# A vision tower with a product-key attention: four dense and four gathered heads in 64 slots, for three and a half and 56

## The reference, cut to what matters

```python
def _pk(x, Wq_pk, pk_keys):                    # 8 heads, 64 keys on each of two sides
    sim = einsum('pbnhd,pkhd->pbnhk', q, pk_keys)
    scores, idx = top_k(sim, 16)               # per side
    index = idx0[:, None] + 64 * idx1[None, :] # 256 pairs
    score = scores0[:, None] + scores1[None, :]
    final_scores, pk_idx = top_k(score, 16)    # 16 rows of 4096 per token and head
    return softmax(final_scores), index[pk_idx]
k = einsum('bnhk,bnhkd->bnhd', kv_scores, keys_table[ind])
v = einsum('bnhk,bnhkd->bnhd', kv_scores, values_table[ind])
sim = einsum('bihd,bjhd->bhij', q, k)          # causal, softmax over 256 tokens
out = softmax(sim) @ v                         # then @ Wo
```

## Time and profile before

| | |
|---|---|
| time, median of 3 runs | 17584.85 us (17558.91 to 17630.44) |
| the profiled execution's own time | 17614.6 us |
| its span, first to last instruction | 17612.8 us |
| granted TensorE clock, mean | 0.823 |
| PE matmuls busy | 13397.9 us (76%) |
| DVE busy | 10470.6 us (59%) |
| POOL busy | 10063.1 us (57%) |
| ACT busy | 7416.4 us (42%) |

### The profile page before, as it was taken

How to read it: one execution, slowest core, us unless ns; L and a number is a source line. 1 busy time by engine, 2 the same in 40 slices (tenths; PEclk the granted TensorE clock), 3 DMA queues, 4 the chain that set the end, 5 groups by cost and what they waited for, 6 DMA issues and landing times.

```text
span 17612.8 us, 261382 instructions
## 1 busy us (share of the span) xinstructions
PE 13397.9 (76%) x71228; PEld 10390.9 (59%) x71228; DVE 10470.6 (59%) x39940; ACT 7416.4 (42%) x17286; POOL 10063.1 (57%) x9220
## 2 busy tenths in 40 slices
PE   4777777777777777777777778777777777777777
PEld 3656556556565555565656656556556665565565
DVE  6656656566566566565665656656656566566562
ACT  2444444444444444444444444444444444344443
POOL 2555555556556556555555556555655555556565
PEclk6888888888888888888888888888888788788888
DMA  2444434444444344343443444444434444344343
GB/s 80 115 114 113 114 108 115 118 110 119 114 112 118 108 115 122 107 116 109 116 117 107 118 111 120 117 113 116 116 108 117 115 112 116 105 116 122 107 116 95
DMA packets 1643030, 1984.06 MB, mean 113 GB/s; under 512 B 527806, under 2 KB 1129022, under 8 KB 1628990
## 3 DMA queue, kind: packets, MB, share of 16 engines
q1 hardware_dynamic: 1346366, 1359.69, 27.2%
q0 software_dynamic: 294912, 604.57, 13.2%
HBM read 1898.00 MB, written 65.01 MB: 111 GB/s over the span
## 4 chain that ended last, share of the span: by engine, by line
PE 38%; another core or an unknown queue 20%; DVE 15%; issue 13%; ACT 8%; DMA 4%; SPq 1%; DVEq 0%; ACTq 0%
PE bank L890 9%; PE bank L926 6%; DMA moving<-keyspace 4%; PE bank L913 4%; ACT bank L1158 3%; PE bank L907 3%; PE bank L767 2%; PE bank L814 2%; PE bank L875 2%; ACT weight L1164 2%; PE bank L896 1%; PE bank L949 1%; PE bank L851 1%; DVE decay L1484 1%
## 5 line engine op out<-in xcount | busy, mean ns | idle before, releaser
L695 POOL DMA_INDIRECT gath<-in_table_dram,rowsT x9216 | 10062.9, 1092 | 7503.4 <-PE bank L926 3775.8
L890 PE MATMUL bank<-weight,rowtab 128*128 128x256 f32 x12288 | 3919.7, 450 | 0.0
L1164 ACT ACTIVATE weight<-bank 128x512 f32<-128x512 f32 x3584 | 2129.3, 594 | 2782.6 <-PE bank L913 1536.2
L890 PEld LDWEIGHTS bank<-weight,rowtab 128*128 128x128 f32 x12288 | 2814.0, 230 | 825.2 <-issue 196.6
L926 PEld LDWEIGHTS bank<-spread,gath 128*128 128x128 f32 x18432 | 2868.0, 223 | 202.3 <-issue 14.5
L913 PE MATMUL bank<-moving,pick_b 96*128 96x512 bf16 x3584 | 1583.5, 442 | 1730.9 <-ACT bank L1158 1282.0
L926 PE MATMUL bank<-spread,gath 128*128 128x96 f32 x18432 | 2773.9, 301 | 15.6 <-issue 15.3
L1158 ACT ACTIVATE bank<-bank,seventeen 128x512 f32<-128x512 f32 x3584 | 2379.1, 664 | 545.9 <-issue 408.5
L907 PE MATMUL bank<-moving,pick_b 96*128 96x512 bf16 x3584 | 1590.2, 444 | 420.4 <-DMA moving<-keyspace 256.4
L913 PEld LDWEIGHTS bank<-moving,pick_b 96*128 96x128 bf16 x3584 | 400.9, 112 | 2268.3 <-ACT bank L1158 1545.6
L1731 DVE TENSOR_REDUCE negmax<-bank 128x1 f32<-128x128 f32 x512 | 147.8, 289 | 2601.6 <-remote 1389.4
(11 more groups left out here) (266 smaller groups left out, 20279.7 us busy)
## 6 DMA issues: line engine op xcount, KB each, us to landing
rowtab<-in_tableD_dram SPq DMA_DIRECT2D x2048, 256.0 KB
wide<-states SPq DMA_DIRECT2D x512, 512.0 KB
moving<-keyspace SPq DMA_DIRECT2D x3072, 64.0 KB
gath<-in_table_dram,rowsT POOLq DMA_INDIRECT x9216
moving<-keyspace SPq DMA_DIRECT2D x3072, 32.0 KB
pix<-in_x_dram SPq DMA_DIRECT2D x64, 1024.0 KB
pix<-in_x_dram SPq DMA_DIRECT2D x128, 512.0 KB
keyspace<-split SPq DMA_DIRECT2D x192, 256.0 KB, 2.0
```

What stands on the lines that cost most here:

```text
L695: pool.indirect_dma_start(out=gath[:, u % RING, j, :], out_offset=None, in_=table, in_offset=bass.IndirectOffsetOnAxis(ap=rowsT[k][:, col: ...
L890: last = mm(dense_ps[:, 0:TOK], rowtab[:, r, s % 2 * 2 + half, :], weight[s % 2][:, half * TOK:(half + 1) * TOK], start=(s % 16 == 0 and h ...
L1164: af(weight[s % 2][:], zd_ps[s % 2][:], ACT.Exp, scale=-1.0).then_inc(weight_ready, 1)
```

## The change

Head 3 becomes fully dense: four dense heads in 16 slots each, 64 slots, and four gathered heads, 32 parts, 128 gathers. The half forms of all helpers go. Windows get eight slots, the ring holds 8 parts (32 gathered tiles), the stream is 80 columns, and a part's sum comes every 61/32 slots, from slot 2 to 61. The three tables of pieces are written anew over 64 slots.

```diff
-DENSE = 3
-GU = UNITS - DENSE * TILES
+DENSE = 4
+DU = DENSE * TILES
+GU = UNITS - DU
 GH = PK_HEADS - DENSE
-DU = DENSE * TILES
-HU = DU + TILES
 SPAN = 32
-SLOTS = 16 * DENSE + 8
+SLOTS = 16 * DENSE
 PART = 4
-PARTS = (GH * SPAN - SPAN // 2) // PART
-RING = 6
-STREAM = 96
+PARTS = GH * SPAN // PART
+RING = 8
+STREAM = 80
...
-ORDER = (1, 2, 3, 4, 0)
-SUMS = [tuple(2 + 12 * g + 3 * i // 2 for i in range(8 if g < 4 else 4)) for g in range(GH)]
+SUMS = [tuple(2 + (8 * g + i) * 61 // 32 for i in range(8)) for g in range(GH)]
...
-WSLOTS = 7
+WSLOTS = 8
...
 47 v.C0
-48 p.S0 v.C1
-49 p.S1
-50 p.S2 v.C2
-51 p.S3 v.C3
-52 p.S4
-53 p.S5
-54 p.S6
-55 p.S7
-56 p.y v.y
-57 p.g a.g
-58 v.g
-59 p.bk
-60 v.h2
+49 v.C1 p.S0
+50 p.S1
+51 v.C2 p.S2
+52 p.S3
+53 v.C3 p.S4
+54 p.S5
+56 p.S6
+57 p.S7
+58 p.y
+59 v.y
+60 p.g a.g
+61 v.g
+62 p.bk
+63 v.h2
...
-35 v.G3 v.re1 a.mi1
-36 v.lo1 p.e0 a.e0
-37 v.G4 v.e2 p.e1 a.e1
-38 v.wg v.e3 p.e2 a.e2
-39 a.wg p.e3 a.e3
-40 v.wh
-41 a.l2
-44 v.R2
-46 v.R3
-47 v.X5 v.wb0
-49 v.R4 v.R5
-50 v.A2 v.A3
-51 v.selh
-52 v.R6 v.R7
-53 v.wb1 v.e4 p.A2 a.hi2
-54 v.R8 v.re2 a.mi2
-55 v.e5 v.lo2 p.e4 a.e4
+36 v.G2
+37 v.e1 v.lo0
+38 v.G3 v.re1 a.mi1
+39 v.lo1 p.e0 a.e0
+40 p.e1 a.e1
+48 v.G4 v.e2
+49 p.e2 a.e2
+50 v.wg v.e3
+51 a.wg p.e3 a.e3
+52 v.wh v.R0
+54 v.R1 v.wb0
+55 v.R2
+56 v.R3 v.A2 v.A3
+57 v.R4
+58 v.R5 v.wb1
+59 v.e4 p.A2 a.hi2
+60 v.re2 v.e5 a.mi2
+61 v.lo2 v.R6 p.e4 a.e4
+62 v.R7 v.wb2 p.e5 a.e5
+63 v.e6 p.A3 a.hi3
...
 OWN = """
-0 p.e5 a.e5
-1 v.R9 v.e6 p.A3 a.hi3
-2 v.re3 v.R0 v.lo3 a.mi3
-3 v.e7 p.e6 a.e6
-4 v.R1 v.wb2 v.wb3 p.e7 a.e7
-10 v.wb4
+0 v.re3 a.mi3
+1 v.lo3 v.e7 p.e6 a.e6
+2 p.e7 a.e7
+7 v.wb3
...
-LOAD_X, STORE_OUT, STORE_2, STORE_3, STORE_0, STORE_BC = 13, 15, 1, 5, 40, 35
+LOAD_X, STORE_OUT, STORE_2, STORE_3, STORE_0, STORE_BC = 13, 15, 63, 3, 52, 35
...
-                if h < DENSE:
-                    last = mm(dense_ps[:, 0:TOK], rowtab[:, r, s % 2 * 2 + half, :],
...
-                else:
-                    for q in (2 * half, 2 * half + 1):
-                        last = mm(dense_ps[:, 0:P], rowtab[:, r, q, :], weight[s % 2][:, q * P:(q + 1) * P],
...
+                last = mm(dense_ps[:, 0:TOK], rowtab[:, r, s % 2 * 2 + half, :],
+                          weight[s % 2][:, half * TOK:(half + 1) * TOK],
...
-                wait(act, s_ready, b * PK_HEADS + (-1, 1, 3, 5, 6)[g])
-                act.wait_ge(summed, b * PARTS + min(8 * (g + 1), PARTS))
...
+                wait(act, s_ready, b * PK_HEADS + (-1, 1, 3, 5)[g])
+                act.wait_ge(summed, b * PARTS + 8 * (g + 1))
...
-                if name in ("sel", "selh"):
-                    lo, hi = (0, DU) if name == "sel" else (DU, HU)
...
+                if name == "sel":
+                    done("L")
```

More of the change, by code:

```diff
@@ L146 @@
 8 p.s0 a.s0
[L147 to L168, removed]
[L169 to L185 removed]
+9 v.T0
+10 v.T1 p.s1 a.s1
+11 v.T2 v.T3 p.s2 a.s2
+12 v.T4
+13 v.T5 v.T6 p.s3 a.s3
+14 v.T7 v.T8
+15 v.T9
+16 v.T10 v.T11
+19 v.T12
+20 v.T13 v.T14
+23 v.T15
+24 v.T16
+25 v.T17 v.T18
+26 v.T19
+27 v.cp v.i v.pr0 a.cp
+28 v.L0
+29 v.L1 v.L2
+30 v.L3 v.wd
+31 v.pr1 a.wd
+32 v.wx v.sel v.A0
+33 v.G0 a.ln p.A0 a.hi0
+34 v.A1 v.G1 v.re0 a.mi0
+35 v.e0 p.A1 a.hi1
+36 v.G2
[18 more added lines that the diff above has]
+63 v.e6 p.A3 a.hi3
 """
 OWN = """
[L189 to L194 removed]
+0 v.re3 a.mi3
+1 v.lo3 v.e7 p.e6 a.e6
+2 p.e7 a.e7
+7 v.wb3
 """
[L198 removed]
+LOAD_X, STORE_OUT, STORE_2, STORE_3, STORE_0, STORE_BC = 13, 15, 63, 3, 52, 35
 LOAD_C = (42, 44, 46, 48)
@@ L644, in period @@
                 for s in range(SLOTS):
-                    if main and s == STORE_2:
-                        store_split(b, k, 2)
+                    if second and s == STORE_2:
+                        store_split(b + 1, 1 - k, 2)
                     if main and s == STORE_3:
@@ L1125, in second @@
                     af(logden[:, 0:DU], wden[:, 0:DU], ACT.Ln).then_inc(den_log, 1)
-                if name == "l2":
-                    act.wait_ge(deng_ready, a + 1)
-                    af(logden[:, DU:], wden[:, DU:HU], ACT.Ln).then_inc(deng_log, 1)
                 if name[:2] == "hi":
@@ L1135, in second @@
                         wait(act, split_stored[side - 1], a * 16)
[L1136 to L1137 removed]
+                    af(split[:, side, 0, :], big_b[:, 0:TOK], ACT.Copy).then_inc(high_ready, 1)
                 if name[:2] == "mi":
@@ L1140, in second @@
                     act.wait_ge(rest_ready, a * 4 + side + 1)
-                    dst, src = (split[:, side, 1, :], rest[:]) if side < 3 else (split_h[:, 1, :], rest[:, 0:P])
-                    af(dst, src, ACT.Copy).then_inc(middle_ready, 1)
+                    af(split[:, side, 1, :], rest[:], ACT.Copy).then_inc(middle_ready, 1)
                 if name[0] == "e":
@@ L1579, in second @@
                                        for u in range(DU)], (0, 2, 3, 5)[what])
-                if name == "X5":
-                    done("G")
-                    done("Gi")
-                    mark["X"] = lists([(pair[:, DU + u, :], pair[:, DU + u, :], fin[:, DU + u, :], None)
-                                       for u in range(TILES)], 5)
                 if name == "wg":
@@ L1604, in second @@
                         done("pr1")
-                    for other in ("sel", "selh"):
-                        if other in mark:
-                            after(mark[other])
+                    done("sel")
                     if "R" in mark:
@@ L1697, in second @@
                     side, t = n // 2, n % 2
-                    for other in ("i", "sel", "selh"):
-                        if other in mark:
-                            after(mark[other])
+                    done("i")
+                    done("sel")
                     wait(dve, count_turned, a * 8 + n - 1)
```

164 lines of the change are left out of this document (59 added, 105 removed).

## The result

The kernel after takes 17,877.4 us (median of 4, 17,866.1 to 17,892.0) against 17,593.5 us of the kernel before on the same chip: ratio 1.0163, interval 1.0137 to 1.0189. Slower by 1.6%, where 17,800 us was forecast. The profiled execution took 17,892.0 us.

A forecast was written before the change was run, and what follows sets the result against it. Bounds: PE's in-order stream, then stalls beside long rows of gathers. Terms 15.7 - 4.3 - 5 - 1 - 2.5 = +2.9 us per image, times 64 = 186, on 17,614.6 gave 17,800 us; range 17,130 to 18,400.

The forecast's parts named there:

- (a): Eight more slots per image, each adding picks, products and ACT passes: +15.7 us per image, 1.96 us per slot.
- (g): Order of gathers in time: shorter rows against one long row at the image's end, -2.5 us per image, bounds -15 and +8.
- (c): Four parts of gathers less per image, 36 to 32, on PE's sums: -4.3 us per image.
- Rival 3: No change: new slots half hidden beside DVE's late third, scan gain worth nothing; 17,620 us, or 17,490; chance 0.20.
- (e): DVE: two row searches less and pieces moved behind the scans, shortening PE's wait for them: -5 us per image, bounds 0 and -7.5.
- (b): Eight half slots become full slots: 0 us per image.
- (d): Matmul stream cut from 96 to 80 columns: 0 us, since width doesn't set the pitch below 128; bounds 0 and +2.
- (f): Attention windows of eight slots instead of seven, so PE's wait for acc goes: -1 us per image.
- The sign that I had named, the unnamed share: Unnamed share of the chain: near 20% for the forecast, under 14% for rival 1, over 22% for rival 2.
- Rival 2: Much slower: ring refilled in one row of 20 to 32 gathers at slots 54 to 62, others standing; 18,470 us, chance 0.12.
- (h): Half head's extras go, key stores move, key loads wait behind the output store: 0, with a loss of up to 2 us.
- rival 1: Faster: short rows of gathers end the stalls, -12 instead of -2.5 us per image; 17,190 us, chance 0.30.

The follow-up runs named there:

- the second kind: Chips on which the unchanged kernel before takes 14,270, 14,308 or 14,339 us; the kernel after took 14,519.2 us there, ratio 1.0150.
- the first kind: Chips on which the unchanged kernel before takes 17,367 us (follow-up group) or 17,593 us (result); the kernel after has ratio 1.0163.
- ring 4: Kernel after with a ring of 4 parts instead of 8: 16,570.3 us, 0.9537 of the kernel before; on the second kind 14,448.4 us, 1.0079.
- the pairs: Kernel after with each even part summed in the slot just before the odd one: 18,029.1 us, 1.0384 of the kernel before, on the first kind.
- the drained kernel: Kernel after with POOL waiting before each part until the part before has landed: 17,312.3 us, 1.2126 of the kernel before, on the second kind.

## Why the prediction was right, point by point

The forecast was 2.9 us per image; the period grew by 4.4. The sign and the size are right, and both were met with luck. By the sum, PE's own work was to grow by 11.4 (a and c) and the waits to fall by 8.5 (e, f, g). By the pages, PE's busy time fell by 4.4 and its idle time grew by 8.7. (Matmul ends are modelled, so the split is rough.) Two terms were far off, (a) and (g), and (g) hid two large ones of opposite sign.

- *(a) eight more slots, (c) four parts less.* A slot with nothing else costs what was said. PE's timeline of the kernel after has, against the earlier trace rows:

```profile
5894.92 0.38 PE L885 MATMUL bank<-moving,pick_b 96*128 96x512 bf16 x1
5896.56 0.38 PE L885 MATMUL bank<-moving,pick_b 96*128 96x512 bf16 x1
```

  1.64 us. But the price taken, 1.96, had a third of the time at the low clock, and the new slots did not add that much. By the groups of lines, picks and products together (L907, L913, L890, L896, then L885, L891, L873) went from 7,692.0 to 8,259.9 us, +8.9 per image where 15.7 was said; on the second kind, 6,964.9 to 7,763.6, +12.5. The sums of gathered rows (L926, then L904) lost 6.4, not 4.3, on the second kind 4.7. The records are shorter at the higher mean clock, a pick 421 ns for 444. The chain has 15.6 us more of PE, but that does not bear (a) out: on the second kind it has 42 more of PE and 33 less of DVE (37 to 55%, 35 to 20%) with the period only 3.3 longer. Rival 3's second half, (e) worth nothing, is wrong, as (e) below shows; how much of (a) is hidden beside DVE no run separates. POOL has 128 gathers per image and is busy 8,747 us (8,950 said).
- *(b)* Half slots for full ones at no cost: no run has it alone.
- *(d) stream.* The chain of the kernel after has the eight matmuls at the full clock, against 0.86 of the earlier trace rows:

```profile
5892.65 0.85 PE bank L904 x8
```

  Sixteen columns less are worth nothing in pitch, as said. By the Trainium skill, "TensorE: Matmul & The Clock Gate", section "Back-to-back issue gap", 80 columns would take 36 ns, an estimate by its formula for a matmul by itself; these records come every 0.106 us. The same section of the Trainium skill says that the formula under-counts few columns in a stream with weight loads, so the prediction held the trace against a figure not meant for it. The measurement decides. What I had bounded at 0 to +2 went the other way: the mean granted clock rose, 0.823 to 0.837, and 0.899 to 0.920 on the second kind. Whether the stream did it was not tried.
- *(e) the scans.* Right, and larger: 479.3 to 40.5 us is 6.9 per image, 7.6 on the second kind (525.6 to 39.2), against 5 said. But "what is late next" was named wrongly: not C1 for S2, but `e2` behind `G4` in slot 49 (284.9 us on the second kind, 4.5 per image) and `ysum` in slot 60 (190.2, 3.0). Together they give nearly all of it back.
- *(f)* PE's wait for `acc`, 83.9 us here and 137.0 on the second kind, is gone on both: 1.3 and 2.1, against 1.
- *(g) the gathers.* Net it was said -2.5. What the first kind adds to the change is +1.1, the period's +4.4 less the +3.3 of the second kind, where no release is late. In it is the late row: ring 4 takes 17 us away, of which 1.6 (0.7%) on the second kind too, so some +15 are the late releases, and some -14 are left for the short rows. No run has the short rows alone, but two more estimates come near: with a ring of 4 on both sides the change is 11.7 faster on the first kind, where the kernel after with ring 4 stands 2 above the kernel before on the second, so -14 (if a ring of 4 costs the kernel before nothing there, which was not run); and the pairs, on the first kind alone, cost 16. Of my bounds, -15 about held and +8 did not. Rival 2's price was wrong because it had the others stand for a third of 25 us. They stand 20 us per image (the 1,308 us) of a row of some 35: DVE's row searches, which I thought would cover it, were over at 6043, with the row a quarter through. The sign that I had named, the unnamed share, is no measure, by the warning above. And the ring has only four places free at slot 53, not eight (the sums of parts 24 to 27 stand in slots 47 to 53); that "four parts are owed at once" is right.
- *(h)* The "loss of up to 2 us" by key loads was too little: PE's wait went from 256.4 to 565.5 us here, 4.8 per image, and from 643.1 to 816.6 on the second kind, 2.7.
- The forecast's own range comes out at 17,470 to 18,200 us from its terms (-2.3 and +9.2 per image), a little wider than the 17,500 to 18,150 given. 17,892 lies in both.

What the second kind adds: with no late releases at all +3.3 us came out, near the +4.4 of the first kind. There eight slots at 1.63 less four parts at 0.86 are +9.6; the waits shown change by -7.6 (scans), -2.1 (acc), -2.5 (rest), +4.5 (one-hot), +3.0 (ysum), +2.7 (keys), +2.9 (over-limit), +0.9 in all, and all of PE's idle time by -0.6, with the small ones. PE's busy time grew by 3.4 (12,055.5 to 12,272.2 us) instead of 9.6. Of the 6 that are missing some go with the higher clock: 0.899 to 0.920 is, by the two levels, 44 to 36 us of an image at the lower one, an estimate of at most 4. The remainder I can't place.

So the figure was right for partly wrong reasons. Of 18,470 us for rival 2 and 17,190 for rival 1, each had its mechanism right and left out the other's.

## What to carry to other kernels

Where a ring is refilled late, the places owed are issued in one row; ask who needs a handover during it. A smaller ring that still covers the latency can be much the better one, as here on the first kind. Before a stall is put down to the program alone, run the same program on a second chip: the same trace place with 0.26 us there and 28 us here is something that no edit shows. When a forecast comes true, hold its terms against the busy and idle times all the same: here both had the other sign. And a piece in the slot right behind its producer is a wait in waiting: five pieces moved by two slots and one load cut in sixteen gave 5%.

## What the runs showed of the hardware that I had not expected

- One program took 17,367 to 17,593 us on some chips and 14,270 to 14,339 on others, 18% less. In the one trace of it on a slower chip 20% of the chain is unnamed, and the granted clock there is 0.82 to 0.83; on the others nothing is unnamed and it is 0.90. Its engines and DMAs are not slower there. What sets a chip, or an occasion, in one kind or the other no run shows.
- On the slower kind the release of DVE and ACT by a PE matmul can be held up for 13 to 29 us beside a row of gathers issued every 1.25 us: in 57 of 64 images, in 35 of these until 0.8 to 5.4 us after the start of the last gather, in 22 not so long. A row of 32 gathers, with DVE at work, on the same kind had no such delay. A gather itself is no slower there (0.94 us, every 1.25 us).
- On the faster kind three of four gathers cost 1.3%: without them the kernel after stands at 1.0021, with all at 1.0150 (on two chips of this kind).
- A part of four gathers with its landing takes 7 to 8 us (the drained kernel, 8.4 per part over the image), so a pause after each can't be hidden.
